# A gather ring of eight groups for four, and one count per two groups from TensorE, in a four-layer graph network

## The reference, cut to what matters

```python
h = relu(layernorm(x))
x = x + segment_sum(h[src] @ weight[etype16], dst)              # layer 0
h = relu(layernorm(x))
x = x + elu(mean_over_edges(h[src]) @ W_l.T + b_l + h @ W_r.T)  # layer 1
h = relu(layernorm(x))
m = silu([h[src], h[dst], edge_attr] @ w1 + b1) @ w2 + b2       # layer 2
x = x + norm(h + mlp([h, segment_sum(m, dst)]))
h = relu(layernorm(x))
a = softmax over a node's edges of q[dst] . key(src, etype8)    # layer 3
x = x + relu(norm(segment_sum(a * (h[src] @ W_r[etype8]), dst)))
```

## Time and profile before

| what | value |
|---|---|
| median of 3 runs | 2771.57 us |
| the profiled execution | 2766.72 us, of which the span is 2764.9 us |
| mean granted TensorE clock | 0.53 of full speed |
| busy: PE, PEld, DVE, ACT, POOL | 1369.1, 1261.2, 739.2, 159.8, 1613.2 us |
| gathers at line 450 | 1248 into `flat` (956 ns each), 416 into `uvT` (974 ns each) |
| stretches of the four loops | 75 to 676, 691 to 1287, 1322 to 1959, 2035 to 2765 us |

### The profile page before, as it was taken

How to read it: one execution, slowest core, us unless ns; L and a number is a source line. 1 busy time by engine, 2 the same in 40 slices (tenths; PEclk the granted TensorE clock), 3 DMA queues, 4 the chain that set the end, 5 groups by cost and what they waited for, 6 DMA issues and landing times.

```text
span 2764.9 us, 21557 instructions
## 1 busy us (share of the span) xinstructions
PE 1369.1 (50%) x5982; PEld 1261.2 (46%) x5982; DVE 739.2 (27%) x2312; ACT 159.8 (6%) x286; POOL 1613.2 (58%) x1693
## 2 busy tenths in 40 slices
PE   6332333333332423233577777677663245655585
PEld 3232323333332323233567777676542235655585
DVE  5211111112311111113222222222421133343456
ACT  3000000000000000001000000000210000000000
POOL 2676666664766667663566666666046666656440
PEclk9555555555555555555655555555655555555555
DMA  6511111111111111110322222222052222222110
GB/s 225 159 25 22 25 23 25 22 24 27 23 24 23 24 23 24 22 25 13 64 57 55 56 57 57 57 57 52 28 219 69 68 61 66 69 57 69 46 46 12
DMA packets 159055, 144.96 MB, mean 52 GB/s; under 512 B 109905, under 2 KB 111855, under 8 KB 158802
## 3 DMA queue, kind: packets, MB, share of 16 engines
q0 software_dynamic: 53888, 69.64, 11.9%
q1 hardware_dynamic: 105058, 73.94, 9.4%
HBM read 113.55 MB, written 37.28 MB: 55 GB/s over the span
## 4 chain that ended last, share of the span: by engine, by line
POOL 28%; another core or an unknown queue 22%; issue 19%; PE 12%; DVE 10%; SPq 7%; DMA 2%; ACT 0%; DVEq 0%; ACTq 0%; POOLq 0%
POOL flat L450 28%; SPq L392 6%; PE ps L1165 3%; PE ps L1156 3%; DVE oh L785 2%; PE ps L1016 2%; DMA table<-flat 1%; DVE ohT L622 1%; PE ps L1003 1%; DVE oh L616 1%; PE ps L1113 1%; PE ps L986 1%; DVE msg L777 1%; PE ps L977 1%
## 5 line engine op out<-in xcount | busy, mean ns | idle before, releaser
L450 POOL DMA_INDIRECT flat<-table,flat x1248 | 1192.9, 956 | 706.6 <-issue 361.1
L1016 PE MATMUL ps<-flat,oh 128*128 128x65 f32 (+1 forms) x1664 | 375.3, 422 | 800.0 <-DVE oh L616 506.0
L1016 PEld LDWEIGHTS ps<-flat,oh 128*128 128x128 f32 x1664 | 360.8, 331 | 814.3 <-issue 814.3
L616 DVE TENSOR_SCALAR oh<-iota_n,drel 128x128 f32<-128x128 f32 x1248 | 261.3, 299 | 1411.8 <-remote 1104.6
L450 POOL DMA_INDIRECT uvT<-table,idx x416 | 405.3, 974 | 330.8 <-issue 122.0
L1156 PE MATMUL ps<-qn,ohT 128*128 x832 | 188.5, 413 | 186.0 <-DVE ohT L622 93.3
L1156 PEld LDWEIGHTS ps<-qn,ohT 128*128 128x128 f32 x832 | 181.7, 325 | 193.5 <-issue 193.4
L1016 PE MATMUL ps<-msg,oh 128*128 128x64 f32 x832 | 186.3, 405 | 140.7 <-issue 113.9
L1165 PE MATMUL ps<-flat,oh 128*128 128x65 f32 x832 | 192.0, 410 | 98.4 <-issue 71.6
L1016 PEld LDWEIGHTS ps<-msg,oh 128*128 128x128 f32 x832 | 179.0, 320 | 135.2 <-issue 135.0
L1165 PEld LDWEIGHTS ps<-flat,oh 128*128 128x128 f32 x832 | 186.4, 329 | 98.8 <-issue 98.7
(11 more groups left out here) (245 smaller groups left out, 722.4 us busy)
## 6 DMA issues: line engine op xcount, KB each, us to landing
table<-flat SPq DMA_DIRECT2D x52, 512.0 KB
drow<-slot_node SPq DMA_DIRECT2D x104, 256.0 KB
flat<-table,flat POOLq DMA_INDIRECT x1248
flat<-edge_attr_padded SPq DMA_DIRECT2D x416, 16.0 KB
uvT<-table,idx POOLq DMA_INDIRECT x416
edge_attr_padded<-edge_attr SPq DMA_DIRECT2D x1, 6250.0 KB
xs<-x SPq DMA_DIRECT2D x1, 768.0 KB
flat<-L_gnn_weight SPq DMA_DIRECT2D x2, 256.0 KB, 3.9
```

Source lines behind the costliest of these rows:

```text
L450: nc.gpsimd.indirect_dma_start(dest[:, b, j, :], None, table, at_).then_inc(gat[b], 16)
L616: last = V.tensor_scalar(oh[:, b, j, :], iota_n[:], drel[:, bass.ds(g * SG + j, 1)], None, ALU.is_equal)
L1016: last = T.matmul(acc[:, bass.ds(n[j] * pitch + shift, width)], oh[:, b, j, :], rows_[:, j, :], start=False, stop=True, skip_group_check=True)
```

## The change

The ring holds eight groups in every layer; in layer 3 it moves from `uvT` into the upper part of `flat`, with a wait before group 6 (`HELD3`) until the node products and the query table are made. `got0` and `got1` now share one tile. The one-hot buffers become one tile of four, of which layers 0 and 1 use all and layers 2 and 3 two for `oh` and two for `ohT` as before. In layers 0 and 1 TensorE counts `used` only after odd groups, by two, and POOL and DVE wait for it only before even groups, each for the odd group that frees both. Layers 2 and 3 count as before.

```diff
-        RING = 4
-        got0 = early(P, [RING, SG, W])
-        got1 = early(P, [RING, SG, D])
-        got3 = uvT[:, 0:RING * SG * 2 * D].rearrange("p (b s d) -> p b s d", b=RING, s=SG)
-        oh = sb("oh", [P, 2, SG, P])
+        RING, AHEAD_OH = 8, 4
+        ring = early(P, [RING * SG * W])
+        got0 = ring.rearrange("p (b s d) -> p b s d", b=RING, s=SG)
+        got1 = ring[:, 0:RING * SG * D].rearrange("p (b s d) -> p b s d", b=RING, s=SG)
+        FREE3 = 2 * P * W + 2 * P * NR
+        got3 = flat[:, FREE3:FREE3 + RING * SG * 2 * D].rearrange("p (b s d) -> p b s d", b=RING, s=SG)
+        assert FREE3 + RING * SG * 2 * D <= SLOTS * (D - 1)
+        oh_all = sb("oh_all", [P, AHEAD_OH, SG, P])
+        oh = oh_all[:, 0:2]
+        ohT = oh_all[:, 2:4]
-        ohT = sb("ohT", [P, 2, SG, P])
...
+        HELD3 = (late - FREE3) // (SG * 2 * D)
...
-            eng.wait_ge(gat[b], (l * NB + 1) * PER + (g - b) * (PER // RING))
+            eng.wait_ge(gat[b], PER * (l * len(range(b, G, RING)) + g // RING + 1))
...
             for g in range(G):
-                if g >= RING:
-                    pool.wait_ge(s("used"), g - RING + 3)
+                if g >= RING and g % 2 == 0:
+                    pool.wait_ge(s("used"), g - RING + 4)
...
-                    if g >= RING:
-                        pool.wait_ge(s("used"), l * G + g - RING + 3)
+                    if g >= RING and (l == 2 or g % 2 == 0):
+                        pool.wait_ge(s("used"), l * G + g - RING + (3 if l == 2 else 4))
...
             for g in range(G):
-                if g == RING - 1:
+                if g == HELD3:
                     pool.wait_ge(s("node_mm"), 20)
+                    pool.wait_ge(s("qn"), 3)
...
             def simple_loop(l):
                 for g in range(G):
-                    dve.wait_ge(s("used"), l * G + g + 1)
-                    onehots(g, g % 2)
+                    if l * G + g >= AHEAD_OH and g % 2 == 0:
+                        dve.wait_ge(s("used"), l * G + g - AHEAD_OH + 4)
+                    onehots(g, g % AHEAD_OH)
...
-            def sum_into_nodes(b, n, rows_, pitch=D, shift=0, width=D):
+            def sum_into_nodes(b, n, rows_, pitch=D, shift=0, width=D, signal=1):
                 for j in range(SG):
-                    last = T.matmul(acc[:, bass.ds(n[j] * pitch + shift, width)], oh[:, b, j, :], rows_[:, j, :], start=False, stop=True, skip_group_check=True)
-                last.then_inc(s("used"), 1)
+                    last = T.matmul(acc[:, bass.ds(n[j] * pitch + shift, width)], oh_all[:, b, j, :], rows_[:, j, :], start=False, stop=True, skip_group_check=True)
+                if signal:
+                    last.then_inc(s("used"), signal)
...
-                        sum_into_nodes(b % 2, n, got0[:, b], PITCH, SHIFT, W)
+                        sum_into_nodes(g % AHEAD_OH, n, got0[:, b], PITCH, SHIFT, W, signal=g % 2 * 2)
                     else:
-                        sum_into_nodes(b % 2, n, got1[:, b])
+                        sum_into_nodes(g % AHEAD_OH, n, got1[:, b], signal=g % 2 * 2)
```

More of the change, by code:

```diff
@@ L218, in network @@
         PAIRS = ("wk1", "w1a", "w1b", "w3a", "wq", "wl", "wr", "w23", "w4", "centre")
-        paired = early(P, [len(PAIRS), P])
-        wqk = early(P, [2 * NR])
-        bqk = early(P, [NR])
         b23 = early(P, [D])
@@ L225, in network @@
         pre2 = early(P, [NT, D])
+        late = taken[0]
+        paired = early(P, [len(PAIRS), P])
+        wqk = early(P, [2 * NR])
+        bqk = early(P, [NR])
+        HELD3 = (late - FREE3) // (SG * 2 * D)
         HALVES = ((0, 16), (16, NT))
@@ L261, in network @@
         INIT, INIT_W = 5, 4
-        NB = G // RING
-        assert G % RING == 0
         def group_of(engine, row_, g, largest):
@@ L283, in landed @@
         def landed(eng, l, g, b):
-            eng.wait_ge(gat[b], (l * NB + 1) * PER + (g - b) * (PER // RING))
+            eng.wait_ge(gat[b], PER * (l * len(range(b, G, RING)) + g // RING + 1))
         BIG, FAR = 1e38, 2.0 ** 20
+        TWICE = 4
         def chunk(eng, c, step):
             for lg in range(PIECES[c]):
-                step(FIRST[c] + lg, lg, lg % RING, PIECES[c] - lg)
+                step(FIRST[c] + lg, lg, (FIRST[c] + lg) % RING, PIECES[c] - lg)
         def summed(c, lg, left):
@@ L299, in summed @@
                 return [lg]
-            once = PIECES[c] - RING
+            once = PIECES[c] - TWICE
             return [FIRST[c - 1] + lg] if lg < once else [FIRST[c - 1] + once + 2 * (lg - once) + k for k in range(2)]
-        assert PIECES == (16, 16, 12, 8) and sum(PIECES) == G and SC == 4 and RING == 4
+        assert PIECES == (16, 16, 12, 8) and sum(PIECES) == G and SC == 4 and TWICE == 4
         NW = 0
@@ L615, in onehots @@
                 for j in range(SG):
-                    last = V.tensor_scalar(oh[:, b, j, :], iota_n[:], drel[:, bass.ds(g * SG + j, 1)], None, ALU.is_equal)
+                    last = V.tensor_scalar(oh_all[:, b, j, :], iota_n[:], drel[:, bass.ds(g * SG + j, 1)], None, ALU.is_equal)
                 last.then_inc(s("oh"), 1)
@@ L792, in step @@
                     for k, w in enumerate(summed(c, lg, left)):
-                        weights_of(w, b if c < 2 or left > RING else k)
+                        weights_of(w, b if c < 2 or left > TWICE else k)
                     score(g, lg, b)
@@ L1174, in step @@
                     for k, (w, n_w) in enumerate(earlier):
-                        weigh(w, w if c < 3 else w - 2 * PIECES[0], b if c < 2 or left > RING else k, n_w)
+                        weigh(w, w if c < 3 else w - 2 * PIECES[0], b if c < 2 or left > TWICE else k, n_w)
                 return step
```

## The result

The changed kernel takes 2838.45 us in the median of 4 runs (2829.21 to 2859.08), the kernel before 2773.12 us (4 runs). The ratio is 1.0248, with an interval from 1.019 to 1.0307: 65 us slower. The forecast was 2853 us. The profiled execution of the changed kernel is the slowest of its four (2859.08 us, span 2857.2), so differences read from the two traces add up to 92 us and not to 65.

A forecast was written before the change was run, and what follows sets the result against it. No engine's work was taken to bound the kernel; POOL pays some 1.45 us of quiet per group. Terms 0 + 0 + 0 + 24 + 30 + 28 = +82 on 2766.7, plus 4.85 for the median, gave 2853 us; range 2740 to 2905.

The forecast's parts named there:

- The pace: First two layers: POOL's pace stays 11.4 to 11.9 us per group whatever the run length; 0 us, bound above +42.
- The law: POOL's gathers: a longer run buys a proportionally longer pause, some 1.45 us of quiet per group.
- Counts and one-hots: First two layers: halving TensorE's counts gives 0 (-20 to 0), one-hots four ahead give 0.
- The tails of the first two layers: Ends of the first two layers: quiet owed and held one-hots delay the last sums, +12 us each, +24 in all.
- The start of the third layer: Third layer: POOL's longer first run delays the first sums 37 to 40 us, about 8 returned; net +30.
- The start of the fourth layer: Fourth layer: TensorE and DVE start scoring three to four groups later, +42, less 14; net +28 (-20 to +60).
- the 14 us given back: Fourth layer: POOL runs on through softmax waits on stocked keys; two thirds of one 21.0 us wait deducted.
- some 30 longer: Sign of being right: the loops of the third and fourth layers each some 30 us longer.
- The faster one: Rival: counts late by their own delay, so eight groups hide it and first-two-layer waits vanish; 2637 us, chance 0.18.
- No change: Rival: pace holds and POOL being ahead pays back longer first runs and tails; 2764 to 2780 us, chance 0.08.
- The starved stream: Rival: weight loads 2.50 us apart slow TensorE's groups in the third and fourth layers; 2931 us, chance 0.08.
- The inference: While POOL issues gathers, other engines' counts drain at a fixed slow rate; while it is quiet, the backlog clears.

The follow-up runs named there:

- depth4_l23: The changed kernel, but in the third and fourth layers POOL waits for the group four before instead of eight; 2779.39 us, ratio 1.0045 to the kernel before.
- depth4_all: The changed kernel with POOL at most four groups ahead in all layers, pair counts and one-hots four ahead kept; 2762.65 us, ratio 0.9965 to the kernel before.
- single_counts: The changed kernel with one count per group again in the first two layers, ring of eight kept; 2842.53 us.
- paced8: The changed kernel, but POOL waits after every group until its gathers have landed; 2775.34 us, ratio 1.0006 to the kernel before.
- mix4448: The changed kernel with four groups ahead in the first three layers, eight in the fourth with a landing wait after each group; 2461.24 us (chip 8), 2462.57 (chip 9).
- four_in_one: The changed kernel at four, eight, three, eight groups ahead; first layer half summed, landing waits per pair in the second, per group in the fourth; 2707.97 us, ratio 0.9781.

## Why the prediction was right, point by point

**The pace (0).** Right. Gathers of the first two layers take 585.7 and 587.0 us against 588.2 and 589.1, and the three further kernels without a landing wait (depth4_l23, depth4_all, single_counts) give 586.6 to 588.8. I had expected runs of six groups with 8.7 us; they are of four, sometimes two, with rests of 3.7 to 5.7, after a first one of ten with 13.92 (10.52 in the second layer). The law holds for the total (132.8 us in the two layers, 130 to 145 forecast) and the length of the runs was wrong. It is also rougher than the prediction has it. Its own show a rest of 11.06 us after four groups, 13.0 us per group, which its list of runs leaves out; and the second layer's first rest after ten groups is 1.05 us per group, the first layer's 1.39. Why the runs are of four was not tested.

**Counts and one-hots (0).** Right within the scatter: single_counts +4 us against the changed kernel, depth4_all -10 us against the kernel before, together with its other edits (forecast 0, bounds -20 to 0).

**The tails of the first two layers (+24).** Measured +9.0 and +13.5 in the profiles. The mechanism is the one priced: in the changed kernel the last gather of the first layer ends at 663.2, TensorE crawls on until 670.1, and the last four groups then take 13.9 us in one go.

```profile
667.27 0.27 PE L1023 MATMUL ps<-flat,oh_all 128*128 128x65 f32 x1 [2.53 <-issue]
667.97 0.27 PE L1023 MATMUL ps<-flat,oh_all 128*128 128x65 f32 x1 [0.43 <-issue]
668.67 0.47 PE L1023 MATMUL ps<-flat,oh_all 128*128 128x65 f32 x1 [0.43 <-issue]
670.07 0.48 PE L1023 MATMUL ps<-flat,oh_all 128*128 128x65 f32 x2 [0.92 <-issue]
671.90 13.91 PE L1023 MATMUL ps<-flat,oh_all 128*128 128x65 f32 x64 [1.35 <-DVE oh_all L622]
```

6.9 + 1.8 + 13.9 is 22.6 us; the forecast's pieces were 8.7 + 14.4 + 2. How much of it shows depends on where the last rest falls: the same ring gave 4.9 and 7.4 us in depth4_l23.

**The start of the third layer (+30).** The delay is there, one group later than forecast, and what is given back was put too small. The prediction moved the first sums by 37 to 40 us and named that as a sign of being right; the first sums, of group 0, start 52.9 us after the first gather instead of 48.1, some 5 us later, and then trickle. It is the sums of group 1 that start 93.7 us after it instead of 57.0, +36.7:

```profile
1399.71 3.03 PE L1023 MATMUL ps<-msg,oh_all 128*128 128x64 f32 x13 [23.21 <-issue]
...
1440.46 3.67 PE L1023 MATMUL ps<-msg,oh_all 128*128 128x64 f32 x16 [0.17 <-issue]
```

Counted from group 1, the giving back was put at 8 us and was 19: the tail grew by 27.5 us, and POOL's gathers took 10.1 us less. The layer is 17.5 us longer, 27.5 in single_counts.

**The start of the fourth layer (+28).** The term that was mis-sized: +50.9 us. The step that failed is the 14 us given back. POOL does run past the softmax after the third piece, where it had waited 21.0 us. But it now waits 23.36 us, until 2569.95, for the softmax after the second piece, and its waits in all stay as they were (110.6 and 110.8 us). What is left is TensorE further behind: four groups would be 4 x 11.9 = 48 us, an estimate by the prediction's own pace. The first weighted sums start 280.6 us after the first gather, before 219.5, and the tail went from 72.1 to 124.1.

The terms that were too high and the one too low nearly cancel: 12 + 12 + 30 + 28 = 82 against 9 + 14 + 18 + 51 = 92 in the profiled executions, and 65 in the medians. The mechanism was right; that the total came so close is partly luck, and of the signs named, the length of the runs, the shift of the first sums and "some 30 longer" for the third and fourth layer did not come true.

**The rivals.** The faster one asked whether the lateness is of a fixed size that eight groups cover. It is not: in the middle of the first layer TensorE's sums end 5 to 21 us after POOL's last gather of the group before the change and 30 to 58 us after it, and the pauses stayed at 67.4 and 65.4 us. The Trainium skill's advice in "DMA: Bandwidth & Descriptors", Rules for kernel authors, to issue a DMA early and wait late, fits chips 8 and 9 in so far as POOL never waits for TensorE at either depth, and there four groups already suffice; on the crawling chips issuing further ahead gained nothing (ratio 1.0248). "No change" came true on chip 9, for a reason that the forecast did not have. Its account, that POOL's lead pays back the starts, is refuted by depth4_l23. The starved stream was half right: TensorE's instructions do stand still one by one, but this raised nobody's pace, and 2931 us was not reached.

**The inference.** The prediction said that the counts of the other engines drain at a slow rate while POOL issues. In the changed kernel more than counts crawls: matmuls and weight loads that wait for nothing take steps of 0.70 us. But depth4_all shows that POOL's rests need only the late counts, 20 us behind sums that were on time.

## What to carry to other kernels

When a producer's pauses are proportional to its runs, a deeper buffer cannot remove them: it only lets the consumer fall further behind, and the price appears at the start and the end of every stage. Compare time per unit over runs of different length before buying depth. Run the kernel before on the same chip each time: the same program took 2384 us on one and 2773 on another, and the landing wait gains 31 us in the fourth layer on one kind (paced8 against before) and costs 76 on the other (mix4448 against the changed kernel).

## What the runs showed of the hardware that was not expected

Whether anything crawls depends on where or when the program runs: the same changed kernel crawls on the first chip and not on chip 9. On the first chip and on chips 11 and 14 TensorE's instructions advance in steps of 0.70 us in many of POOL's runs of indirect DMAs, on chips 8 and 9 not. How much of it shows depends on the program: TensorE's "issue" idle time before the first layer's sums is 374.9 us in the changed kernel, 89.4 before and 25.9 in depth4_all, while POOL's rests there stay at 67 to 71 us in all three. POOL's gather takes 0.94 us and the gap 0.30 on both kinds. The granted clock is also the same (0.532 and 0.533). Whether it is the chip itself, its host or a condition of the moment is open, and so is the resource that TensorE and SP share with POOL's gathers; four_in_one points to the gathers as what mainly fills it, at 1.3 to 1.4 us of quiet per eight of them.

The Trainium skill ("Trainium Architecture — The Big Picture", Inside one NeuronCore) says that each engine has its own instruction stream, runs in parallel and meets the others only through semaphores. On chips 8 and 9 the traces agree; on the crawling chips they do not quite: in the changed kernel TensorE spent 374.9 us of the first layer in gaps that no semaphore in the profile explains.
